# A cross-attention and FP4 feed-forward kernel: fourteen written-out batches become a loop of seven rounds on every engine

## The reference

```python
x = x + xattn(layernorm(x), ctx)        # 16 heads of 16, softmax(Q K^T / 4) V, then @ Wo + bo
x = x + ffn(layernorm(x))               # fp4_linear(silu(fp4_linear(h, w_gate)) * fp4_linear(h, w_up), w_down)
# fp4_linear: both operands rounded in blocks of 16 to an FP4 grid, scale = max|block| / 6; inner width 704
```

## Time and profile before

| | us |
|---|---|
| three runs | 3777.43, 3782.05, 3784.6 (median 3782.05) |
| the profiled execution, its own time | 3777.43 |
| its span, first to last instruction | 3775.6 |
| PE busy | 3599.6 (95% of the span) |
| DVE busy | 2984.2 (79%) |
| ACT busy | 2242.8 (59%) |
| POOL busy | 871.0 (23%) |
| mean granted TensorE clock | 0.992 |

### The profile page before, as it was taken

How to read it: one execution, slowest core, us unless ns; L and a number is a source line. 1 busy time by engine, 2 the same in 40 slices (tenths; PEclk the granted TensorE clock), 3 DMA queues, 4 the chain that set the end, 5 groups by cost and what they waited for, 6 DMA issues and landing times.

```text
span 3775.6 us, 57225 instructions
## 1 busy us (share of the span) xinstructions
PE 3599.6 (95%) x19654; PEld 1643.5 (44%) x19654; DVE 2984.2 (79%) x6641; ACT 2242.8 (59%) x4350; POOL 871.0 (23%) x920
## 2 busy tenths in 40 slices
PE   7999999999999999999999999999999999999997
PEld 3334444444453444435444444444534444354434
DVE  6887787887777887777877877878778877778874
ACT  2666566666656556566566666666566565656662
POOL 2221212222122222122212122222122222222113
PEclk9999999999999999999999999999999999999998
DMA  2222121121211122121121211212111221211100
GB/s 67 51 50 53 24 59 34 36 54 34 51 36 42 41 42 49 29 48 39 39 55 24 60 33 35 53 36 50 35 43 40 44 49 28 49 39 38 38 22 7
DMA packets 148034, 156.44 MB, mean 41 GB/s; under 512 B 58129, under 2 KB 118818, under 8 KB 147746
## 3 DMA queue, kind: packets, MB, share of 16 engines
q1 hardware_dynamic: 147746, 152.78, 18.6%
HBM read 39.53 MB, written 8.39 MB: 13 GB/s over the span
## 4 chain that ended last, share of the span: by engine, by line
PE 75%; DVE 15%; ACT 4%; DMA 2%; issue 2%; SPq 1%; POOL 0%; POOLq 0%; ACTq 0%
PE out_ps L815 17%; PE score_ps L804 16%; PE piece_ps L829 16%; PE work L770 8%; DVE piece_max L1097 6%; PE work L745 5%; PE work L737 5%; PE work L780 4%; ACT probs L914 4%; DMA x_in<-in_x 2%; PE work L760 1%; PE work L724 1%; PE work L754 1%; PE work L729 1%; DVE neg_parts L1012 1%
## 5 line engine op out<-in xcount | busy, mean ns | idle before, releaser
L1097 DVE TENSOR_REDUCE piece_max<-piece_ps 128x1 f32<-128x400 f32 (+1 forms) x4096 | 2134.0, 566 | 537.3 <-PE piece_ps L829 519.5
L914 ACT ACTIVATE probs<-score_ps 128x512 f32<-128x512 f32 (+1 forms) x3328 | 1876.3, 598 | 1021.7 <-PE score_ps L804 1016.6
L829 PE MATMUL piece_ps<-k_stack,q_stack 96*128 96x400 bf16 (+1 forms) x4096 | 1282.7, 336 | 67.1 <-DVE piece_max L1097 59.5
L804 PE MATMUL score_ps<-q_stack,k_stack 99*128 99x512 bf16 (+1 forms) x3328 | 1258.5, 385 | 48.7 <-ACT probs L914 14.4
L815 PE MATMUL out_ps<-probs,v_ones 128*17 128x512 f32 x6656 | 878.0, 599 | 2.1 <-ACT probs L914 1.0
L804 PEld LDWEIGHTS score_ps<-q_stack,k_stack 99*128 99x128 bf16 (+1 forms) x3328 | 324.4, 98 | 879.7 <-ACT probs L914 642.3
L829 PEld LDWEIGHTS piece_ps<-k_stack,q_stack 96*128 96x128 bf16 x4096 | 396.8, 98 | 649.9 <-DVE piece_max L1097 430.6
L1152 POOL TENSOR_TENSOR h<-h,h_grid 128x704 f32<-128x704 f32 (+1 forms) x68 | 111.3, 1637 | 1081.7 <-DVE h_grid L966 1081.7
L770 PE MATMUL work<-wgu_T,xq_T 128*128 128x256 f32 (+1 forms) x1440 | 345.3, 361 | 0.4 <-ACT xq_T L886 0.4
L770 PEld LDWEIGHTS work<-wgu_T,xq_T 128*128 128x128 f32 x1440 | 258.8, 189 | 48.6 <-ACT xq_T L886 3.4
L815 PEld LDWEIGHTS out_ps<-probs,v_ones 128*17 128x17 f32 x6656 | 110.3, 95 | 279.7 <-issue 235.1
(11 more groups left out here) (139 smaller groups left out, 2588.7 us busy)
## 6 DMA issues: line engine op xcount, KB each, us to landing
k_stack<-k_parts SPq DMA_DIRECT2D x1536, 50.0 KB, 2.2
q_stack<-q_parts SPq DMA_DIRECT2D x1536, 16.0 KB, 1.8
ctx_in<-in_ctx SPq DMA_DIRECT2D x48, 384.0 KB, 3.6
x_in<-in_x SPq DMA_DIRECT2D x16, 512.0 KB, 4.5
resid<-in_x SPq DMA_DIRECT2D x16, 512.0 KB, 4.5
out<-y SPq DMA_DIRECT2D x64, 128.0 KB, 2.0
q_stack<-neg_rows SPq DMA_DIRECT2D x192, 4.0 KB, 1.7
ctx_in<-in_ctx SPq DMA_DIRECT2D x16, 48.8 KB
```

The source lines that it names most:

```text
L804: pe.matmul(score_ps[0:r, n % SCORE_RING, :], k_stack[:, par, slot(g, j), m * P:m * P + r], q_stack[:, par, slot(g, j), :], start=True, st ...
L829: pe.matmul(piece_ps[:, n % PIECE_RING, 0:hi - lo], q_stack[0:SROWS, par, slot(g, j), t * P:(t + 1) * P], k_stack[0:SROWS, par, slot(g, j) ...
L914: act.activation(probs[0:r, step % 2, j, :], score_ps[0:r, (PER_GROUP * m + j) % SCORE_RING, :], ACT.Exp, scale=SCORE_SCALE).then_inc(prob ...
L1097: dve.tensor_reduce(piece_max[:, row, c:c + 1], piece_ps[:, n % PIECE_RING, 0:piece_at[c + 1] - piece_at[c]], AX_X, ALU.max).then_inc(piec ...
```

## The change

The fourteen middle batches are no longer written out one behind the other. Each engine gets a loop of seven rounds, and its body holds two batches (two, since several buffers change by the parity of the batch). Batches 1 to 14 are computed as before, in the same order on each engine.

```diff
         def run(eng, body):
 
             body("first", (None, 0))
-            for b in range(1, B - 1):
-                body("middle", (None, b))
+            with eng.Fori(0, (B - 2) // 2) as i:
+                body("middle", (i, 1))
+                body("middle", (i, 2))
             body("last", (None, B - 1))
             body("tail", (None, B))
```

## The result

| | before | changed kernel |
|---|---|---|
| median, us | 3779.74 (3774.06 to 3784.6, 4 runs) | 3817.35 (3812.8 to 3818.9, 4 runs) |
| ratio | | 1.0098 [1.0081, 1.0115] |
| profiled execution: time, span | 3777.4, 3775.6 | 3817.06, 3815.3 |

The changed kernel is 37.6 us slower. The forecast was 3816 us, slower, and the time lies 1.4 us from it; as a difference, 34 us were forecast. That looks better than it is: as the following rows show, the branches back cost nearly three times what the forecast gave them, the register arithmetic less than it gave, and parts that are in no term of the sum go both ways.

A forecast was written before the change was run, and what follows sets the result against it. PE was taken to bound the kernel. The profiled 3777.4 us + 13 (branches) + 20 (register arithmetic) + 1 (addresses) = 3811; with the median 4.6 above that execution, 3816 us, 8-in-10 range 3786 to 3900.

The forecast's parts named there:

- That PE is the bound and a pause on it comes out of the time: Middle batches: PE busy 3109.7 of 3206 us; any holdup beyond its queued work adds directly to the time.
- Term 1: Branches back between batches: engines stand 3.4 us for the target's fetch, less 1.2 for x; six cost 13 us (0 to 20).
- The 1.2 us that x was to give back: At each branch back SP loses only 2.2 us, so x comes 1.2 us earlier against PE and DVE's wait vanishes.
- Term 2: Register arithmetic before PE's waits: 680 per batch at 51 ns, mostly covered by 903 us of stops; 20 us uncovered.
- The price of 20 ns for a round's opening: PE's 71 round openings per batch, 14 batches: arithmetic that doesn't fit, 20 ns each, 20 us.
- Term 3: SP's register addresses for x, resid, context and store: only x is on the path, 1 us (0 to 3).
- The sequencer as the bound: Rival, 0.25: above about 95 ns per wait PE's stops no longer cover the arithmetic; above 3850 us, near 3916 with two instructions.
- No change: Rival, 0.12: fetch under 2 us and arithmetic fully covered; at most 6 us, 3782 to 3788.
- faster: Rival, 0.06: SP goes on while PE pauses under 1.2 us, x comes on time; gain at most 7 us, 3775.
- Wrong if the period between seams grows by more than 5 us: Sign in the profile after: such growth between branches back at batch boundaries would mean the sequencer is to blame.

The follow-up runs named there:

- The announcement: Changed kernel with `hint_back_edge=True`, a hint at each round's head to fetch the branch target early: all engines 3789.98 us, PE alone 3803.25, all but PE 3815.9.
- the kernels with extra matmuls: Changed kernel with four or eight more fp32 matmuls of 512 columns queued on PE at each round's end: four 3805.09 us, eight 3815.23 us.
- The written-out register kernel: Changed kernel without loop or branch: seven pairs of batches written out, register set anew for each pair; 3786.28 us, 1.0021 of the kernel before.
- the chains: Written-out register kernel with each PE wait's value worked out afresh in its own register: 3794.17 us; with two more additions per wait 3805.83 us, 1.0069.
- the kernel with two branches: Changed kernel with batches 1 to 8 written out with constants and the loop over the last six only; 3795.67 us, 1.0043 of the kernel before.

## Why the prediction was right, and where it was not

The time came out right by luck: the seams cost 25 us more than forecast, and errors the other way made up for it. Step by step:

**That PE is the bound and a pause on it comes out of the time: right.** The announcement on all engines but PE gains nothing (3815.9), on PE alone 14 us.

**Term 1, six branches back at 2.2 us, 13 us: the mechanism right, the size off by a factor of three.** The measured cost is 6.3 us each, 37.6 us. The pause itself was well bounded: 3.4 us forecast, 3.4 to 4.1 in PE's branch record, 3.3 to 3.9 idle, a restart 3.1 us late where 3.4 - 1.2 was said. Of the forecast's two parts, the packet's 1.15 us is right (0.9 to 1.4), and the 2.2 us around it are 2.4 to 2.9. What the sum left out stands behind the restart. PE's granted clock was 0.50 for 7 to 10 us, which costs some 3 us more; this is the step that the sum had at nothing. The trace of before had the warning, in the first batch, where I had not looked. PE idles 2.27 us and then 3.40, and the score behind it takes 0.58 us at a clock of 0.55; timeline and window of the kernel before:

```profile
76.83 0.22 PE L749 MATMUL work<-ident,neg_parts 128*128 128x128 bf16 x1 [2.27 <-DVE neg_parts L1018]
...
80.44 0.58 PE L804 MATMUL score_ps<-q_stack,k_stack 99*128 99x512 bf16 x1 [3.40 <-DMA q_stack<-neg_rows]
```

```profile
77.00:88.00 11.00, 7.61 (x24) 1.87 (x24) 3.36 (x6) 4.10 (x8) 0.00 (x0) 0.55 0.27 71
```

A pause of 3.4 us was just what I forecast for each seam, and 0.58 us for a score instead of 0.39 was its second price. That announcing the branch takes the whole 6.3 us off a seam (and leaves 1.6 us on the batch behind it) is shown; the division, 3.1 for the pause and some 3 for the clock, rests on the kernels with extra matmuls and on the seams of one kernel at which the clock fell or held.

The 1.2 us that x was to give back are there as a wait: behind a seam DVE no longer stands for x (no wait at 770.66, against 1.25 in the earlier trace rows). In the time it is less: the batches behind a seam take 0.6 us less than the average before.

That the engine stands at the branch until its target lands, for which the forecast had no row, is borne out: 3725 ns with and 357 ns without that wait, and the packet is in the trace (16 KB for PE's; those of q14 are of 8). Where the branch falls through, its record is 40 to 88 ns, against 3.7 us where PE's waits.

**Term 2, register arithmetic, 20 us: too high, by how much is open.** The written-out register kernel shows 4 us in the middle batches, and that is close to what two builds can differ by. At equal waits for x my estimate is 9 to 13 us; no run shows it alone. Three numbers under it were off: 7210 instructions, not 9520; 32 ns each, not 51; and the stops did not shrink. The price of 20 ns for a round's opening had no row behind it and is not seen.

**Term 3, addresses, 1 us: right.** Register addresses alone change the time by 0.06% [-0.03, 0.15].

**Not in the sum: +6.7 us in the last batch and its tail, +2.5 at the entry, -7.1 in the fourteen batches beside the seams' cost.** The first two are in the main late copies of the maxima with the clock's fall behind them, seen without a loop too. The last goes with x: in 500 to 3300 us DVE waits for it 20.9 us in 13 batches before, 1.6 each, and 3.0 us in 6 after, 0.5 each and none behind a seam; the kernel with the written-out registers keeps 17.5 us in 13 and has no gain, the one with x issued first has no wait and batches of 227.3. By the line of the kernel before, 18 us less of wait in the fourteen batches are worth some 20 us, where the forecast gave x 7 us; the -7.1 would then be those 20 less the 13 for the registers. This division is an estimate. Behind the seams x is early since PE is late; in between its transfer is shorter (3.7 us in the median from issue to landing, against 4.5), and why is open.

**The rivals.** The sequencer as the bound, given 0.25, fell by the chains: with 108 ns per wait the kernel is 0.7% slower than before, not 3.5%. No change and faster both needed a pause of PE under about 1.2 to 2 us; it idled 3.3 us or more at all six seams.

**What the profile was to show.** Six seams with a common idle time and none between: so it is. Batches without a branch within 2 us of 228.6: 228.1 to 229.0. "Wrong if the period between seams grows by more than 5 us": 457.9 us before, 234.7 + 228.4 = 463.1 after, 5.2 more, so by my own mark the sequencer was to blame. It wasn't, and the mark was ill chosen: a seam that costs more moves that period just as arithmetic does. PE's idle time, said to grow by 20 us, grew by 6 in the middle stretch (3246.0 - 3143.7 = 102 against 96); the six pauses add 18 us (21.7 less 0.56 for each before), and the idle time before pieces fell from 46.4 to 35.0.

## What to carry to other kernels

Here the cost of the hardware loop stood at its branch back, on the engine that bounds the kernel: 6.3 us each time. So price the wait for its target (3.7 us at PE's branch), and then what the clock does behind the pause, by what PE's matmuls take after gaps of that length elsewhere in the trace (here 0.58 us for a score instead of 0.39 behind a gap of 3.40). Try the announcement on all engines, not one: on all it gained 27 us, on PE alone, where PE then stood up to 2.0 us at a seam for ACT, 14, and on all but PE nothing. And look at the loop's end, where the wait came once (3.20 us of PE idle, 6.6 us of time). Register arithmetic in front of waits was cheap here (4 us net, 9 to 13 by the estimate), and a load issued too late, which the same seam shows, was worth 23 us.

## What was not expected of the hardware

- An engine's stall at a branch back is in PE's record (3.7 us) but not in those of SP and ACT (54 and 45 ns), which stood all the same: SP 3.0 us from its branch to its next issue, ACT 2.6 us with only PE's branch announced.
- With the branch announced, the wait appears where the loop ends instead: 3.20 us of PE idle and 6.6 us of time, once.
- PE's branch record is longer with matmuls queued ahead of it: 4.7 us (5.1 at most) with eight records queued, 3.7 (4.1) without. The packets tell why, as in the kernel with two branches, where one branch took 5.3: with eight, the next packet in order starts 0.3 to 0.5 us behind the branch, the target's starts behind it at 0.9 to 1.0, and side by side that one takes 2.1 to 2.7 us.
- TensorE's granted clock fell to 0.50 at six seams of six after 3.3 to 3.9 us without work, and with four extra matmuls ahead of the branch at two of six, after 1.60 and 1.25 us; at the other four, after 1.09 to 1.65 us, it held.
- Eight extra fp32 matmuls of 512 columns ran as sixteen records, one every 0.43 us.
